# The mixed stage of a two-layer attention and expert network, with relative products, layer 1's chain and the experts' groups in another order

## The chip, the cores and the metric

The kernel runs on one core of a Trainium2 chip. The time is device microseconds (us) of one launch, median of three executions. The engines of a core are TensorE (PE in the profile, its weight loads PEld), VectorE (DVE), ScalarE (ACT), GpSimd (POOL) and SyncE (SP), which issues most DMAs. Each takes its instructions strictly in the order of its own program and waits on semaphores for the others.

## What is computed

Eight images of 32x32 tokens with 96 channels pass through a layer 0 (attention with relative position terms), a layer 1 (causal attention) and four experts, of which each token uses two:

```
x = x + conv_attn(group_norm(x))          # qkv, softmax(q k^T * scale + rel_h + rel_w) v, proj
t = t + causal_attn(layer_norm(t))        # layer 1, 6 heads of 16
scores = einsum('bsd,de->bse', x, gate_w) + gate_b       # x is now layer_norm(t)
probs  = softmax(scores); keep the top 2 of 4, divide by their sum
h = gelu(einsum('bsd,edh->ebsh', x, w1) + b1)            # 4 experts, 96 -> 384
y = einsum('ebsh,ehd->ebsd', h, w2) + b2                 # 384 -> 96
t = t + einsum('bse,ebsd->bsd', masked, y)
```

## The kernel before

One image (1024 tokens) is one element; the program is pipelined over the eight elements. For each element there is layer 1's attention (`attention(it, 1)`), the next element's layer 0 attention (`attention(it, 0)`), and then a **mixed stage**, `mix`, in which three strands of three elements run side by side:

- **rel** and **val0**, layer 0 two elements on: two groups of values (`val`), and eight relative products (`bias`, matmuls at L548 and L550, eight to a product). ScalarE copies each product out in two pieces (L980, L981), VectorE subtracts in two pieces (L1326) and frees the buffer.
- **a**, the experts of the current element: the gate (`gate_scores` L707, then `gates` on VectorE, with an Exp on ScalarE at L1012); twelve groups of `up` (L715, Gelu on ScalarE at L997) and `down` (L729), three of each to an expert; after an expert's third `down` ScalarE adds the bias (`expert_out`, L1005), TensorE transposes the result (`back`, L746) and VectorE adds it (`expert_add`, L1308).
- **next_mix**, layer 1's chain of the next element: `ln` (Ln and Exp of the softmax sums on ScalarE, L969 and L971), `den` (three steps on VectorE, L1216 to L1219), `res` (output projection L691, then residual and statistics on VectorE, L1231 to L1252), `nrm` (Ln and Exp at L869 and L871, four small steps and eight normalizing ones on VectorE, L1154 to L1258), `tr` (transposes L699, copy L986), `qk` (projections L528, ScalarE L883, VectorE L1194), `val`, `lev` (splitting in bf16 levels, L899, L1075, L1349), a write to DRAM and a read back by SyncE, and sixteen row **maxima** of layer 1's first two heads (`first_maxima`: L759 and a mask at L762, VectorE reduces at L1299).

There are nine mixed stages. Six (elements 0 to 5) hold all three strands, of which five are the turns of a hardware loop; the first of all has no experts, that of element 6 has no relative products and no val0, and the last has the experts only.

The order of the stage is one hand-written list, `MIX`; every engine walks it and executes its own part of each item. So a step that waits on one engine holds back all that stands behind it in the list on that engine. Each product, `up`, `res`, `tr`, `qk`, `val` and maximum writes a buffer of `psT`, of which there are two, used in turn (`take_mixed`): a fill waits until the fill two before it has been read, by ScalarE (`ta_free`) for `up`, `tr`, `val` and `val0`, by VectorE (`t_free`) for the others. `down` and the gate have banks of their own (`psS`, `psM`). `back` writes over the gate's bank, and the first one waits for `gates` to have finished (`m_free`). A `down` waits for its Gelu (`ta_free`). ScalarE's Gelu is in another function table than Ln and Exp; the compiler puts an ACT_TABLE_LOAD ahead of a function whose table isn't loaded.

## Time and profile before

| | before |
|---|---|
| median of 3 executions | 2429.63 us (2428.53 to 2431.78) |
| the profiled execution | 2437.21 us, of which the span is 2435.4 us |
| mean granted TensorE clock, share of 2.4 GHz | 0.878 |
| TensorE (PE) busy | 2016.1 us, 83% |
| VectorE (DVE) busy | 1238.8 us, 51% |
| ScalarE (ACT) busy | 1102.1 us, 45% |
| DMA, mean | 46 GB/s |

The profile gives for each engine the sum of its busy time. The trace gives single instructions in order of time, equal ones merged into a row; behind a row stands, in brackets, how long the engine had been idle and whose work ended that. The view of stages gives, for a stretch of time, how long each engine was busy in it and which clock TensorE was granted: 1.00 is 2.4 GHz, 0.50 is 1.2 GHz. The stage that is followed below is the mixed stage of the third turn of the loop, from 1083.92 us (its first val0 matmul) to 1179.59 us (the first matmul of the next attention).

### The profile page before, as it was taken

Reading aid. Unit: us, or ns where it says so; the run is one execution under the profiler, and the core shown is the slowest. Engines: PE = TensorE matmul, PEld = TensorE weight load, DVE = VectorE, ACT = ScalarE, POOL = GpSimd, SP = SyncE. Lnnn points to the kernel's source line nnn. Section 1 sums busy time; section 2 is a strip of 40 time slices with the busy share of each in tenths; the row PEclk is TensorE's granted clock in tenths of the full one; section 3 lists DMA queues with packets and bytes.
Section 4 is the critical chain, followed back from the end, with each engine's and each line's share of the span. In section 5 each row is a group of like instructions: output and inputs, shape, how many; then the busy total and the mean of one; then the engine's idle time right before and its main releaser. Section 6 shows DMA issues by size and latency. Waiting matters only on the chain.

```text
span 2435.4 us, 28956 instructions
## 1 busy us (share of the span) xinstructions
PE 2016.1 (83%) x9408; PEld 804.7 (33%) x9408; DVE 1238.8 (51%) x2512; ACT 1102.1 (45%) x1408; POOL 141.5 (6%) x68
## 2 busy tenths in 40 slices
PE   1389578898889988889788988889888898899858
PEld 0123222343323432334323433334323343234324
DVE  5453466454654555635664445545566355643522
ACT  0325434563445633465344643456344653455333
POOL 0000000100010000200011000100002000100010
PEclk9589669988899888999799888998899998999888
DMA  1704420243004230061202430033300621000300
GB/s 40 130 1 84 70 46 16 57 74 71 7 15 95 36 73 11 25 112 45 37 16 57 74 72 6 16 83 48 73 10 26 108 48 31 16 10 5 65 14 7
DMA packets 55740, 111.43 MB, mean 46 GB/s; under 512 B 17686, under 2 KB 18903, under 8 KB 54040
## 3 DMA queue, kind: packets, MB, share of 16 engines
q1 hardware_dynamic: 54040, 109.06, 23.2%
q8 instruction: 89, 1.46, 0.3%
q14 instruction: 75, 0.61, 0.1%
q10 hardware_dynamic: 1536, 0.30, 0.1%
HBM read 61.82 MB, written 34.60 MB: 40 GB/s over the span
## 4 chain that ended last, share of the span: by engine, by line
issue 61%; PE 21%; DVE 7%; POOL 4%; DMA 3%; SPq 2%; ACT 2%; POOLq 0%; DVEq 0%; ACTq 0%
PE psOM L612 4%; PE psS L563 4%; DVE mx L1205 4%; PE psT L591 2%; PE psT L592 2%; PE psS L729 2%; PE psT L715 2%; PE psT L594 1%; POOL split L1075 1%; PE psT L528 1%; SPq L395 1%; DMA scr<-qb 1%; DMA kb<-scr 1%; PE psT L759 1%; POOL lb L1082 1%
## 5 line engine op out<-in xcount | busy, mean ns | idle before, releaser
L944 ACT ACTIVATE probs<-psT 128x1024 f32<-128x1024 f32 (+7 forms) x768 | 624.2, 836 | 659.7 <-PE psT L592 362.5
L1205 DVE TENSOR_REDUCE mx<-psS 128x1 f32<-128x512 f32 (+3 forms) x1152 | 685.7, 641 | 461.9 <-PE psS L563 370.1
L592 PE MATMUL psT<-qb,kb 97*128 97x512 f32 x768 | 415.2, 615 | 0.0
L612 PE MATMUL psOM<-probs,v 128*32 128x512 f32 (+3 forms) x2688 | 394.2, 570 | 12.8 <-ACT probs L944 12.8
L563 PE MATMUL psS<-ka,qa 128*128 128x512 bf16 x768 | 280.1, 409 | 91.2 <-DVE mx L1205 82.4
L591 PE MATMUL psT<-qa,ka 128*128 128x512 bf16 x768 | 314.7, 410 | 29.0 <-DMA qb<-negr 28.4
L715 PE MATMUL psT<-xf,w1s 97*128 97x512 f32 x384 | 208.5, 675 | 1.6 <-DVE mrow L1299 1.6
L1326 DVE TENSOR_TENSOR qb<-psT,qa 32x768 fp32r<-32x768 f32 x128 | 121.4, 948 | 154.5 <-ACT qa L980 152.7
L729 PE MATMUL psS<-probs,w2s 128*96 128x512 f32 x384 | 192.2, 625 | 4.6 <-ACT probs L997 4.6
L997 ACT ACTIVATE probs<-psT 128x1024 f32<-128x1024 f32 x96 | 98.1, 1023 | 196.7 <-PE psT L715 196.4
L594 PE MATMUL psT<-qr,kr 97*128 97x512 bf16 (+3 forms) x576 | 183.2, 362 | 2.8 <-ACT probs L944 0.9
L563 PEld LDWEIGHTS psS<-ka,qa 128*128 128x128 bf16 x768 | 61.9, 99 | 352.4 <-DVE mx L1205 268.7
L592 PEld LDWEIGHTS psT<-qb,kb 97*128 97x128 f32 x768 | 162.5, 212 | 20.9 <-issue 2.4
L563 PE MATMUL psS<-kr,qr 96*128 96x512 bf16 (+3 forms) x384 | 137.0, 397 | 35.3 <-DVE mx L1205 31.2
L591 PEld LDWEIGHTS psT<-qa,ka 128*128 128x128 bf16 x768 | 77.8, 101 | 217.3 <-issue 134.5
L1299 DVE TENSOR_REDUCE mrow<-psT 128x1 f32<-128x128 f32 (+7 forms) x128 | 92.8, 755 | 91.3 <-PE psT L762 91.3
L612 PEld LDWEIGHTS psOM<-probs,v 128*32 128x32 f32 x2688 | 68.3, 109 | 143.9 <-issue 89.2
L759 PE MATMUL psT<-kr,qr 96*128 96x512 bf16 (+1 forms) x192 | 68.7, 440 | 56.7 <-DMA kr<-scr 30.4
L715 PEld LDWEIGHTS psT<-xf,w1s 97*128 97x128 f32 x384 | 78.3, 214 | 91.8 <-issue 78.7
L1075 POOL TENSOR_TENSOR split<-resid,split 96x1024 bf16<-96x1024 f32 x16 | 34.1, 2130 | 1224.2 <-ACT split L899 1224.2
L729 PEld LDWEIGHTS psS<-probs,w2s 128*96 128x96 f32 x384 | 63.4, 173 | 98.7 <-issue 93.4
L1308 DVE SCALAR_TENSOR_TENSOR x<-psOM,g,x 128x96 f32<-128x96 f32 x256 | 60.4, 307 | 68.7 <-PE psOM L746 68.5
(140 smaller groups left out, 1742.3 us busy)
## 6 DMA issues: line engine op xcount, KB each, us to landing
scr<-split SPq DMA_DIRECT2D x32, 576.0 KB, 4.3
scr<-qb SPq DMA_DIRECT2D x16, 768.0 KB, 4.8
qr<-scr SPq DMA_DIRECT2D x48, 192.0 KB, 6.6
au<-ot SPq DMA_DIRECT2D x192, 32.0 KB, 2.0
lb<-ot SPq DMA_DIRECT2D x192, 32.0 KB, 2.0
qr<-scr SPq DMA_DIRECT2D x48, 128.0 KB, 4.3
kr<-scr SPq DMA_DIRECT2D x48, 128.0 KB, 7.3
qa<-scr SPq DMA_DIRECT2D x32, 128.0 KB, 3.8
```

Of the source, the lines that this page charges most:

```text
L563: last = mm(bank[:, 0:n], q[0:rows, h, t * P:(t + 1) * P], k[0:rows, h, kc * HALF:kc * HALF + n], start=True, stop=not diagonal)
L591: mm(o[:, a:b], ka[:, h, ks], qa[:, h, a:b], start=True, stop=False)
L592: last = mm(o[:, a:b], kb[:, h, ks], qb[:, h, a:b], start=False, stop=True)
L594: last = mm(o[:, a:b], kr[:, h, ks], qr[:, h, a:b], start=True, stop=a != q0)
L612: last = mm(psO[j:j + 2 * HD, a - c * HALF:HALF], v[:, kt, 2 * p + hh, :], probs[:, (2 * kt + hh) % 4, a:(c + 1) * HALF], start=kt == 0, s ...
L715: last = mm(o[:, c * HALF:(c + 1) * HALF], w1s[:, a:a + P], xf[:, c * HALF:(c + 1) * HALF], start=True, stop=True)
L729: last = mm(psS[0:C, c, :], w2s[:, n, :], hbuf[:, n % 4, c * HALF:(c + 1) * HALF], start=j == 0, stop=j == HJ - 1)
L759: last = mm(o[:, c * HALF:c * HALF + n], q[0:rows, h, t * P:(t + 1) * P], k[0:rows, h, c * HALF:c * HALF + n], start=True, stop=not diagonal)
L944: A(probs[:, n % 4, q0:T], psT[:, t_slot(ts, m), q0:T], ACT.Exp).then_inc(t_free, 1)
L997: A(hbuf[:, n % 4, :], psT[:, t_slot(stage, fill), :], ACT.Gelu).then_inc(ta_free, 1)
L1205: V.reduce_max(mx[layer][:, p % 2, (h % 2) * NT + t, kc:kc + 1], psS[:, s_bank(st, fill), 0:max_cols(layer, t, kc)], AX).then_inc(s_free, 1)
L1326: ins = V.tensor_tensor(rest[0], rest[1], lead[0], ALU.subtract)
```

## The change

`MIX` is written in another order. The first six relative products no longer stand together: the list now begins rel 0, up 0, rel 1, up 1, rel 2, down 0, rel 3, and layer 1's `ln` stands behind rel 3 instead of behind rel 5. The gate moves from ahead of the first `up` to behind up 6. Ahead of the q and k projections stand ten of the experts' 24 groups, where there were thirteen; the gate and the first `back` move behind them. Between the projections and the maxima stand eight groups (seven before), and among the maxima six (three before), with two `back`s (one before); the last `back` stands behind maximum 11 instead of maximum 7.

Two waits go with it. The first `up` now waits for VectorE's copy of its input (`s_free`), which the gate did before; and ScalarE preloads the table of Ln and Exp at `ln`, since a Gelu now stands ahead of it.

```diff
-MIX = ([("val0", 0), ("val0", 1)] + [("rel", g) for g in range(6)]
-       + [("ln", 0), ("gate", 0), ("up", 0), ("up", 1), ("den", 0), ("down", 0), ("up", 2), ("rel", 6), ("down", 1), ("res", 0),
...
-       + MAXES[:2] + [("up", 11)] + MAXES[2:4] + [("down", 10)] + MAXES[4:6] + [("down", 11)] + MAXES[6:8] + [("back", 3)]
-       + MAXES[8:])
+MIX = ([("val0", 0), ("val0", 1), ("rel", 0), ("up", 0), ("rel", 1), ("up", 1), ("rel", 2), ("down", 0), ("rel", 3), ("ln", 0),
+        ("up", 2), ("rel", 4), ("down", 1), ("den", 0), ("rel", 5), ("up", 3), ("res", 0), ("down", 2), ("rel", 6), ("up", 4),
+        ("nrm", 0), ("down", 3), ("rel", 7), ("tr", 0), ("up", 5), ("qk", 0), ("qk", 1), ("val", 0), ("lev", 0), ("val", 1),
+        ("up", 6), ("gate", 0), ("down", 4), ("up", 7), ("back", 0), ("down", 5), ("up", 8), ("down", 6), ("up", 9), ("down", 7),
+        ("back", 1)]
+       + MAXES[:2] + [("down", 8)] + MAXES[2:4] + [("up", 10)] + MAXES[4:6] + [("down", 9), ("back", 2)] + MAXES[6:8]
+       + [("up", 11)] + MAXES[8:10] + [("down", 10)] + MAXES[10:12] + [("down", 11), ("back", 3)] + MAXES[12:])
...
             def up(it, stage, n):
 
+                if n == 0:
+                    pe.wait_ge(s_free, upto("s_free", it, stage, 0))
...
                     elif what == "ln":
+                        exp_table()
                         den(it, "mix")
```

The lines of the changed kernel are two or three further down than the same lines before (L715 becomes L717, L997 becomes L999, L1299 becomes L1302). Three places show what moves, all from the mixed stage of element 0, which has the same order as the loop's. First ScalarE around `ln`, before. L980 and L981 are a relative product's two copies, L969 and L971 are `ln`, L1012 is the gate's Exp, L997 a Gelu and the load of its table:

```order
L980 ACTIVATE qa<-psT 32x4x6x32
L981 ACTIVATE qa<-psT 32x192x4
L969 ACTIVATE il<-lb 96x1024
L971 ACTIVATE il<-il 96x1024
L1012 ACTIVATE g<-g 128x32
L997 ACT_TABLE_LOAD
L997 ACTIVATE probs<-psT 128x1024 x3
```

The same place on ScalarE after the change:

```order
L982 ACTIVATE qa<-psT 32x4x6x32
L983 ACTIVATE qa<-psT 32x192x4
L876 ACT_TABLE_LOAD
L971 ACTIVATE il<-lb 96x1024
L973 ACTIVATE il<-il 96x1024
L999 ACT_TABLE_LOAD
L999 ACTIVATE probs<-psT 128x1024
L982 ACTIVATE qa<-psT 32x4x6x32
L983 ACTIVATE qa<-psT 32x192x4
```

`ln` now stands between two table loads, with up 2's Gelu and rel 4's copies behind it. In a whole mixed stage ScalarE has seven table loads where it had three.

Second TensorE around the output projection L691, before, with the semaphores that each row waits for (rel 6 is ahead of these rows; L729 is a `down`, L715 an `up`):

```order
L729 MATMUL psS<-probs,w2s 96x512 [waits ta_free]
L729 MATMUL psS<-probs,w2s 96x512
L691 MATMUL psT<-wp,att 128x96 [waits ta_free,att_ready]
L691 MATMUL psT<-wp,att 128x96 x7
L715 MATMUL psT<-xf,w1s 128x512 [waits t_free]
L715 MATMUL psT<-xf,w1s 128x512
```

And after (rel 5 is ahead of these rows; L717 is up 3, L731 is down 2):

```order
L717 MATMUL psT<-xf,w1s 128x512 [waits t_free]
L717 MATMUL psT<-xf,w1s 128x512
L691 MATMUL psT<-wp,att 128x96 [waits t_free,att_ready]
L691 MATMUL psT<-wp,att 128x96 x7
L731 MATMUL psS<-probs,w2s 96x512 [waits ta_free]
L731 MATMUL psS<-probs,w2s 96x512
```

The projection's buffer was freed by ScalarE (`ta_free`, up 2's Gelu); now VectorE frees it (`t_free`, rel 5), behind `den`.

Third VectorE at the end of the stage, before: L1308 is an expert's addition (eight steps), L1299 the reductions of the maxima.

```order
L1349 TENSOR_TENSOR split<-il,split 96x1024
L1308 SCALAR_TENSOR_TENSOR x<-psOM,g,x 128x96 x16
L1299 TENSOR_REDUCE mrow<-psT 128x1 x8
L1308 SCALAR_TENSOR_TENSOR x<-psOM,g,x 128x96 x8
L1299 TENSOR_REDUCE mrow<-psT 128x1 x8
```

And after:

```order
L1311 SCALAR_TENSOR_TENSOR x<-psOM,g,x 128x96 x16
L1302 TENSOR_REDUCE mrow<-psT 128x1 x6
L1311 SCALAR_TENSOR_TENSOR x<-psOM,g,x 128x96 x8
L1302 TENSOR_REDUCE mrow<-psT 128x1 x6
L1311 SCALAR_TENSOR_TENSOR x<-psOM,g,x 128x96 x8
L1302 TENSOR_REDUCE mrow<-psT 128x1 x4
```

Two of the experts' additions now stand among the maxima where one did.

## Rows read from the trace of the kernel before

**Rows 1.** The page: busy time, share of the span, instructions of each engine.

```profile
PE 2016.1 (83%) x9408; PEld 804.7 (33%) x9408; DVE 1238.8 (51%) x2512; ACT 1102.1 (45%) x1408; POOL 141.5 (6%) x68
```

**Rows 2.** Stages: from:to, length, busy of each engine, clock, DMA share, GB/s.

```profile
1085.90:1097.80 11.90, 8.51 (x50) 3.22 (x49) 8.60 (x10) 8.47 (x11) 0.00 (x0) 0.72 0.63 114
1097.80:1105.40 7.60, 7.60 (x23) 5.30 (x23) 6.05 (x18) 5.61 (x7) 0.00 (x0) 0.53 0.03 2
1105.40:1133.70 28.30, 28.30 (x101) 13.04 (x100) 15.27 (x43) 16.37 (x20) 0.00 (x0) 1.00 0.00 1
1133.70:1155.00 21.30, 18.75 (x70) 9.14 (x69) 8.45 (x19) 10.14 (x12) 2.12 (x1) 1.00 0.37 103
1155.00:1177.20 22.20, 17.29 (x60) 6.65 (x60) 13.29 (x24) 2.39 (x3) 0.00 (x0) 0.68 0.62 100
```

**Rows 3.** Order of time, first relative products: start, length, instruction, idle before.

```profile
1085.87 0.26 PE L548 MATMUL psT<-qr,relt 96*32 96x192 bf16 x1
...
1087.37 0.80 ACT L980 ACTIVATE qa<-psT 32x768 bf16<-32x768 f32 x1 [0.90 <-PE psT L550]
...
1088.20 3.85 DVE L1326 TENSOR_TENSOR qb<-psT,qa 32x768 fp32r<-32x768 f32 x4 [7.40 <-ACT qa L980]
...
1090.16 0.26 PE L548 MATMUL psT<-qr,relt 96*32 96x192 bf16 x1 [1.54 <-DVE qb L1326]
```

**Rows 4.** Order of time, ScalarE: `ln`'s second step, and the table load of `nrm`.

```profile
1100.62 1.06 ACT L971 ACTIVATE il<-il 96x1024 f32<-96x1024 f32 x1
...
1123.04 1.28 ACT L874 ACT_TABLE_LOAD   x1
1124.33 0.21 ACT L869 ACTIVATE sm<-sm 128x8 f32<-128x8 f32 x1
```

**Rows 5.** Order of time: a `down`, an `up`, its Gelu, a `back` at full clock.

```profile
1106.56 1.88 PE L729 MATMUL psS<-probs,w2s 128*96 128x512 f32 x4
...
1108.28 1.88 PE L715 MATMUL psT<-xf,w1s 97*128 97x512 f32 x4
...
1110.20 1.02 ACT L997 ACTIVATE probs<-psT 128x1024 f32<-128x1024 f32 x1 [2.41 <-PE psT L715]
...
1123.51 0.83 PE L746 MATMUL psOM<-cst,xg 96*128 96x96 f32 x8
```

**Rows 6.** Order of time, layer 1's chain; the first row from the first mixed stage.

```profile
271.48 3.73 PE L691 MATMUL psT<-wp,att 97*128 97x96 f32 x16 [5.30 <-DVE att L1219]
...
1108.01 1.22 DVE L1219 SCALAR_TENSOR_TENSOR att<-il,au 96x1024 f32<-96x1024 f32 x1
...
1113.27 1.92 PE L691 MATMUL psT<-wp,att 97*128 97x96 f32 x16
...
1118.48 0.17 DVE L1252 TENSOR_SCALAR sm<-sm 128x8 f32<-128x8 f32 x1
...
1125.62 2.01 DVE L1258 TENSOR_SCALAR xn_tok<-x,sm 128x96 f32<-128x96 f32 x8
```

**Rows 7.** Order of time, the gate on TensorE and the last step of `gates`.

```profile
1097.78 3.58 PE L707 MATMUL psOM<-gw,xf 97*128 97x4 f32 x16
...
1105.18 0.19 DVE L1291 TENSOR_TENSOR g<-g,gden 128x32 f32<-128x32 f32 x1
```

**Rows 8.** Order of time, TensorE, the first of the maxima.

```profile
1154.98 0.23 PE L759 MATMUL psT<-kr,qr 96*128 96x128 bf16 x1 [2.55 <-DMA kr<-scr]
```

**Rows 9.** Order of time, VectorE in the maxima: an addition and four reductions.

```profile
1168.77 1.88 DVE L1308 SCALAR_TENSOR_TENSOR x<-psOM,g,x 128x96 f32<-128x96 f32 x8
...
1173.03 1.73 DVE L1299 TENSOR_REDUCE mrow<-psT 128x1 f32<-128x640 f32 x2 [0.25 <-PE psT L762]
1174.98 2.24 DVE L1299 TENSOR_REDUCE mrow<-psT 128x1 f32<-128x896 f32 x2 [0.22 <-PE psT L762]
```

**Rows 10.** Order of time, element 6's mixed stage: `ln`, and the first reductions.

```profile
2211.05 1.06 ACT L969 ACTIVATE il<-lb 96x1024 f32<-96x1024 f32 x1 [6.34 <-DMA lb<-ot]
...
2264.08 0.62 DVE L1299 TENSOR_REDUCE mrow<-psT 128x1 f32<-128x128 f32 x2 [2.69 <-PE psT L762]
```

More of the change, by code:

```diff
@@ L69 @@
 MAXES = [("max", i) for i in range(2 * NT)]
-MIX = ([("val0", 0), ("val0", 1)] + [("rel", g) for g in range(6)]
-       + [("ln", 0), ("gate", 0), ("up", 0), ("up", 1), ("den", 0), ("down", 0), ("up", 2), ("rel", 6), ("down", 1), ("res", 0),
-          ("up", 3), ("down", 2), ("rel", 7), ("up", 4), ("down", 3), ("nrm", 0), ("back", 0), ("up", 5), ("down", 4),
-          ("up", 6), ("tr", 0), ("down", 5), ("up", 7), ("qk", 0), ("qk", 1), ("down", 6), ("val", 0), ("lev", 0), ("val", 1),
-          ("back", 1), ("up", 8), ("down", 7), ("up", 9), ("down", 8), ("up", 10), ("back", 2), ("down", 9)]
-       + MAXES[:2] + [("up", 11)] + MAXES[2:4] + [("down", 10)] + MAXES[4:6] + [("down", 11)] + MAXES[6:8] + [("back", 3)]
-       + MAXES[8:])
+MIX = ([("val0", 0), ("val0", 1), ("rel", 0), ("up", 0), ("rel", 1), ("up", 1), ("rel", 2), ("down", 0), ("rel", 3), ("ln", 0),
[5 more added lines that the diff above has]
+       + [("up", 11)] + MAXES[8:10] + [("down", 10)] + MAXES[10:12] + [("down", 11), ("back", 3)] + MAXES[12:])
 def there(stage, kind):
```

## The prediction, made before the changed kernel ran

> **What bounds the kernel now.** I read the page first, then the stages of one turn, then the order of time within them. TensorE is busy 83% of the span, VectorE 51% and ScalarE 45% [rows 1], so TensorE's time is the kernel's time, and the question is where it idles or runs at the lower clock. In the mixed stage that is two places [rows 2]. In the six relative products (1085.9 to 1097.8) TensorE works 8.5 of 11.9 us, and its clock falls from 1.00 to 0.50 there, so that the gate and the first two `up`s behind them run at 0.53. From the first maximum to the last (1155.0 to 1177.2) it works 17.3 of 22.2 us at a mean clock of 0.68. In between lie 28 us without a gap at 1.00, and a wait of 2.55 us for layer 1's keys to come back from DRAM [rows 8]. The change puts experts' groups into both thin places. The two weak places cost at most some 3.4 us of idle time, 3.5 us of low clock, 2.6 us of waiting and 5 us idle among the maxima; what has to be asked is what the new neighbours wait for.
>
> **Prices.** A relative product takes TensorE 1.3 us. The first one starts at 1085.87, ScalarE's two copies of 0.80 start 1.50 us later, VectorE's two subtractions (1.92 us, half of the 3.85) end at 1090.12, and TensorE takes the buffer again at 1090.16, 4.29 us after the start [rows 3]. An `up` or `down` takes 1.72 us at full clock (1106.56 to 1108.28), and the Gelu starts 1.92 us after its `up` and lasts 1.02; a `back` takes 0.8 [rows 5]. A table load takes 1.28 us and the next instruction starts 0.01 later [rows 4]. `ln` is two steps of 1.06 [rows 4]. `den` is three steps of 1.22, so 3.7 us; `res` takes TensorE 1.8 us at full clock (1113.27) and 3.7 at half (271.48), and residual and statistics end 3.6 us after its matmuls (1115.03 to 1118.65); `nrm` takes VectorE 2.8 us, the last 2.01 of them in one row [rows 6]. `gates` ends 4.0 us after the gate's last matmul (1101.36 to 1105.37); that gate took 3.58 us at half clock, so I take 1.9 at full [rows 7]. An expert's addition takes 1.88 us [rows 9]. The last four of a head's eight reductions take 1.73 and 2.24 a pair [rows 9].
>
> **Part 1, up to the projections of q and k.** I lay the new order out by these prices, from 0 at the first val0 matmul (1083.92); a fill can't start before the fill two places ahead of it is read. Products at 1.95, 6.24 and 10.53 alternate with `up`s at 3.25 and 7.54: TensorE waits 1.27 us ahead of each, because a pair of product and `up` fills 3.0 of the 4.29 us. That is no better than two products in 4.3 us before, only more work in it. Rel 3 runs at 13.55, up 2 at 14.85. Now ScalarE: rel 3's copies end at 16.7; then load, Ln, Exp, load (4.7 us), so up 2's Gelu ends at 22.4, rel 4's copies, which wait behind it though their matmuls ended at 19.1, at 24.1, and VectorE is done with rel 4 at 25.2. `den` follows (to 29.0), then rel 5's subtractions (to 30.9). The output projection needs `den` and the buffer of rel 5: it starts at 31.0, while rel 5 and up 3, the last work ahead of it, ended at 27.0. So TensorE does 3.0 us of work from 20.9 to 31.0. Then `res` to 32.7, down 2, rel 6, up 4, down 3 and rel 7 to 40.5. Up 4's Gelu, the load and Ln/Exp of `nrm` end at 40.4, VectorE's `nrm` at 43.3, `tr` starts there (2.8 us of waiting), rel 7 is freed at 45.2, up 5 runs to 47.0, and the projections start at 47.0. Before they started at 49.8 (the edge of the stages at 1133.7, [rows 2]), but with three more groups (5.2 us), the gate and a `back` done.
>
> **Part 2, to the first maximum.** The projections take 3.4 us, the two `val`s 1.9 and 1.5 of waiting for VectorE, since no `down` stands between them any more; then eight groups (13.8), the gate (1.9) and two `back`s (1.6). The first `back` waits for `gates`: VectorE starts these after `lev`, which ends at 57.1, and the gate's Exp has ended by 58.4, so `gates` is done at 61.7 and TensorE idles 0.8. Sum 25.0: the first maximum starts at 72.0. Before it started at 71.1 (1154.98) [rows 8]. The transfer took 21.3 us from the projections [rows 2, 8], so the data is there at 68.3 and the 2.55 us wait is gone; what takes its place is TensorE's own work. At full clock this half is 0.9 us longer.
>
> **Clock of part 1.** In the relative products before, the clock fell after stretches in which TensorE worked 8.5 of 11.9 us [rows 2]. The stretch from 20.9 to 31.0 is much emptier (3.0 of 10.1), so I take the low clock for `res` (+1.9 by the 3.7 us at 271.48 [rows 6]) and for down 2 (+1.7, double its 1.72); both lie on the chain to `nrm`. That is +3.6. Bounds: 0 if the clock holds, and +5.4 if it has fallen already in the first pairs, which adds up 2's and down 1's delay to `ln`'s chain.
>
> **Part 3, the maxima.** Before, 22.2 us at a mean clock of 0.68 [rows 2]. After, from 0 again: back 1's addition first (to 2.0), maxima 0 and 1, down 8, maxima 2 and 3; up 10 waits for max 2's reduction (3.5 to 5.2); max 5 waits for up 10's Gelu (6.4); down 9, back 2, maxima 6 and 7 to 10.3; but VectorE does the addition first (to 11.4), so up 11 gets its buffer at 12.6; max 9 waits for up 11's Gelu (15.6); down 10, maxima 10 and 11, down 11 to 19.7; back 3 waits 1 us for ScalarE's `expert_out`, which stands directly ahead of it, and ends at 21.5; then the addition (23.5) and the last four reductions (0.8 + 0.9 + 2.24) to 27.6. So +5.4 us. VectorE's own work is 13.3 us [rows 2] plus two more additions, 17.1; TensorE has six groups and two `back`s, 12 us, beside the maxima: the two buffers make them take turns instead of overlapping. Ends: +2.4 if some 3 us of these turns overlap after all, and 3.4 more than my value if up 11 and down 10 run at half clock; I take neither, since the maxima now start out of dense work.
>
> **The added table loads.** Four per stage, 5.1 us of ScalarE; two are in `ln`'s 4.7 us above, one in `nrm`'s. First the row: from the load at 1123.04 the next instruction starts at 1124.33 [rows 4]. The Trainium skill, page "ScalarE: Activation LUTs", section "What ACT_TABLE_LOAD costs", gives 1283 ns for the load, as this trace, but 2.66 us for a switch with its drain, and its rules say to do all of one set before switching, which speaks against this change. By its figure the three loads on the chain would cost 4.1 us more a stage; this trace doesn't bear out the drain.
>
> **Sum.** A full stage: 0.9 + 3.6 + 5.4 = +9.9, six times: +59.4. The first stage has no groups; its chain starts two products earlier but pays a load: -1. In element 6's stage `ln` waits 6.34 us for its DMAs [rows 10] with the gate's Exp and two Gelus queued behind it; these Gelus now come first. The same count gives the first maximum 8.1 us earlier than before (reductions from 2264.08 [rows 10]), less 3 for low clock after `nrm`'s wait, and +5.4 in the maxima: +0.3. The last stage: the first `back` waits 0.6 for `gates`: +0.6. Total +59.3. The profiled execution was 2437.2, which gives 2496.5; it lies 7.6 above the median of 2429.6, so the median comes to 2489.
>
> **Rivals.** (a) The same waits but the clock holds in part 1: for it, `up`s are dense work and 28 us of groups ran at 1.00 [rows 2]; against it, the ten empty us. Six times 6.3, -1, -2.7, +0.6: +34.7, so 2464. (b) The clock falls in the first pairs and among the maxima too, where 0.68 stands now [rows 2]: six times (1.8 + 3.4) = 31 more: 2520. (c) Faster: the pairing works as meant. VectorE would have to get through `den` and rel 5 without TensorE waiting, so that of part 1's waits only the 1.27s and the 0.8 of `tr`'s buffer are left: 7 us less and no low clock, 0.9 + 5.4 - 7.7 = -1.4 a stage, with -3 elsewhere -11: 2418. It decides on whether the wait ahead of `res` and `tr` together stays under 0.5 us; `ln`'s 4.7 us on ScalarE [rows 4] speak against it. (d) A switch costs more than its row: if each of the three loads on the chain held ScalarE as long again as its 1.28, 3.8 us in each of 7 stages: 27 more, 2516; against it, the start 0.01 us behind the load [rows 4]. (The Trainium skill's page on ScalarE, same section, would make it so.) (e) Nothing measurable, where the gains in clock balance the maxima: 2430.
>
> **How the numbers follow.** Forecast 0.50, (a) 0.22, (b) 0.12, (c) 0.10, (d) 0.02, (e) 0.04. The range takes the forecast, (a) and (b) with some room for the size of the stage terms: 2450 to 2523; it leaves out (c) and (e). 0.2% is about what a measurement of this kernel can tell from no change. Faster 0.10, same 0.04, slower 0.86.
>
> **What would show it.** In the changed trace of a loop's stage: waits of TensorE of about 1.3 us for VectorE's subtraction ahead of rel 1, 2 and 4; some 4 us idle ahead of L691, ended by VectorE; about 2.8 ahead of L699; no wait for a DMA at the first maximum, and that maximum 75 to 76 us after the first val0; 27 to 28 us from first to last maximum; clock 0.5 around L691. I am wrong if the projection's wait is under 1 us, or if the maxima take less than 24 us.

## The result, and the profile after

The changed kernel takes 2536.0 us (median of 4 runs, 2529.1 to 2545.8), the kernel before on the same chip 2430.7 (2428.5 to 2432.2): a ratio of 1.0437 with a 95% interval of 1.0401 to 1.0473. The direction is the forecast one, but the loss is 105 us where 59 were worked out, and the time lies 13 us above the range. The profiled executions span 2527.2 and 2435.4 us.

The page's line of busy times stands beside [rows 1]: TensorE is busy for 29 us more in 92 us more span, VectorE the same, ScalarE 44 us more (31 table loads more, 1.28 us each, are 40 of these).

```profile
PE 2045.4 (81%) x9408; PEld 803.0 (32%) x9408; DVE 1239.4 (49%) x2512; ACT 1146.2 (45%) x1439; POOL 141.6 (6%) x68
```

I follow element 2's stage, that of [rows 2] (the third of the six full stages, and the second turn of the loop, not the third as is said ahead of the prediction). It begins with the first val0 matmul, at 1083.92 before and 1107.61 after; times with a plus sign count from there. First the windows of the kernel before (from:to, length, busy time of TensorE, weight loads, VectorE, ScalarE and GpSimd, granted clock, DMA share, GB/s): up to the first maximum, and the whole stage up to the transpose of the maxima. Then the same of the changed kernel, with the maxima between.

```profile
1083.92:1154.98 71.06, 65.12 (x254) 32.57 (x253) 38.36 (x89) 41.67 (x51) 2.12 (x1) 0.90 0.25 54
1083.92:1179.60 95.68, 82.43 (x315) 39.25 (x313) 51.67 (x113) 44.06 (x54) 2.12 (x1) 0.84 0.33 63
```

```profile
1107.61:1186.17 78.56, 65.89 (x234) 30.33 (x233) 34.67 (x73) 44.89 (x52) 2.13 (x1) 0.87 0.28 56
1186.17:1216.50 30.33, 21.88 (x82) 8.90 (x80) 16.99 (x40) 4.78 (x6) 0.00 (x0) 0.84 0.29 53
1107.61:1219.04 111.43, 87.76 (x314) 39.24 (x313) 51.67 (x113) 49.67 (x58) 2.13 (x1) 0.85 0.28 54
```

The stage grew by 15.75 us with the same matmuls in it. TensorE's busy time grew by 5.3 of these, its idle time by 10.4 (13.25 to 23.67). The mean granted clock of the stage is nearly what it was (0.84 and 0.85): the low clock lies at other places, and for longer in all. So the clock explains only part of the 5.3. The rest fits the rows ahead of waits: an `up` there shows 1.98 us of busy time, where in a dense stretch the next instruction starts after 1.72, and there are more waits now. It wasn't split further. By halves: 71.06 to 78.56 us up to the first maximum, 22.24 to 30.33 from there to the last reduction.

The order of time of TensorE in that stage (start, length, instruction, idle time ahead of it and what ended it), changed kernel:

```profile
1113.85 0.26 PE L548 MATMUL psT<-qr,relt 96*32 96x192 bf16 x1 [0.92 <-DVE qb L1329]
...
1133.15 3.78 PE L717 MATMUL psT<-xf,w1s 97*128 97x512 f32 x4 [1.31 <-DVE qb L1329]
1138.85 3.73 PE L691 MATMUL psT<-wp,att 97*128 97x96 f32 x16 [1.92 <-DVE qb L1329]
1142.37 3.36 PE L731 MATMUL psS<-probs,w2s 128*96 128x512 f32 x4
...
1154.83 1.27 PE L699 MATMUL psT<-cst,xn_tok 128*96 128x128 f32 x8 [2.70 <-DVE xn_tok L1261]
1156.70 3.78 PE L717 MATMUL psT<-xf,w1s 97*128 97x512 f32 x4 [0.59 <-DVE qb L1329]
...
1186.17 0.22 PE L761 MATMUL psT<-kr,qr 96*128 96x128 bf16 x1
...
1198.61 2.50 PE L717 MATMUL psT<-xf,w1s 97*128 97x512 f32 x4 [2.06 <-DVE mrow L1302]
...
1202.53 3.67 PE L731 MATMUL psS<-probs,w2s 128*96 128x512 f32 x4
```

Three things are to be seen. Rel 1 starts at +6.24, the output projection (L691) at +31.2, and ahead of them TensorE waits for VectorE's subtractions; up 3, between rel 5 and the projection, already runs at half clock (3.78). The projection and down 2 behind it take 3.73 and 3.36 us, where before they took 1.92 and 1.88; up 5, behind the wait for `nrm`, takes 3.78 too. The first maximum waits for no DMA any more, but among the maxima down 10 takes 3.67 us, and up 11 ahead of it 2.50, the lower clock again.

Element 1's stage, from 806.73, shows that the low clock doesn't come at the same places every time. TensorE from the first pairs to the maxima:

```profile
814.35 3.78 PE L717 MATMUL psT<-xf,w1s 97*128 97x512 f32 x4
...
819.45 3.73 PE L731 MATMUL psS<-probs,w2s 128*96 128x512 f32 x4
...
840.55 3.73 PE L691 MATMUL psT<-wp,att 97*128 97x96 f32 x16 [1.92 <-DVE qb L1329]
...
858.66 3.78 PE L717 MATMUL psT<-xf,w1s 97*128 97x512 f32 x4
...
888.67 0.22 PE L761 MATMUL psT<-kr,qr 96*128 96x128 bf16 x1
...
901.11 1.98 PE L717 MATMUL psT<-xf,w1s 97*128 97x512 f32 x4 [2.06 <-DVE mrow L1302]
```

and VectorE's last reductions in it:

```profile
912.12 4.14 DVE L1302 TENSOR_REDUCE mrow<-psT 128x1 f32<-128x640 f32 x4
```

Here up 1 and down 0 run at half clock among the first pairs, and the first maximum comes at +81.9 instead of +78.6. Up 11 takes 1.98 us behind the same wait of 2.06, so the maxima run at the full clock nearly to their end and take 27.6 us, not 30.3. In the six full stages, in order, the first maximum comes at +82.2, 81.9, 78.6, 82.0, 78.2 and 79.5 (mean 80.4; before 71.7), and the maxima take 29.3, 27.6, 30.3, 27.6, 30.3 and 30.3 us (mean 29.2; before 22.0).

The table gives the length of every mixed stage, from ScalarE's last copy of the attention's output to its copy of `negb` for the next attention (the last stage: to the end of the span), in us:

| | first | el. 0 | 1 | 2 | 3 | 4 | 5 | el. 6 | last |
|---|---|---|---|---|---|---|---|---|---|
| before | 73.9 | 96.3 | 95.2 | 96.1 | 97.0 | 94.3 | 93.8 | 82.4 | 89.7 |
| after | 73.6 | 112.0 | 112.9 | 111.8 | 112.4 | 111.4 | 110.2 | 83.3 | 88.5 |

A full stage has gone from 95.4 to 111.8 on average: +16.4, six times 98. The first, element 6's and the last changed by -0.3, +0.9 and -1.2. What is left, some -6, lies outside the mixed stages, in parts that the change doesn't touch. The profiled execution is also the fastest of the changed kernel's four (2529.1, the others up to 2545.8), so the medians stand 105 apart and the two profiles 92.

### The profile page after: what moved, and what is told of

The parts are those of the page before. It is cut to its first block, busy times and chain, and to the rows that moved or that the text cites. A ratio compares the mean times of both kernels' runs of the same rounds, so it can differ in the third digit from the quotient of the medians.

```text
span 2527.2 us, 28993 instructions
## 1 busy us (share of the span) xinstructions
PE 2045.4 (81%) x9408; PEld 803.0 (32%) x9408; DVE 1239.4 (49%) x2512; ACT 1146.2 (45%) x1439; POOL 141.6 (6%) x68
## 4 chain that ended last, share of the span: by engine, by line
PE 63%; DVE 17%; ACT 6%; issue 6%; DMA 5%; SPq 1%; POOL 1%; DVEq 0%; POOLq 0%; ACTq 0%
PE psOM L612 12%; PE psS L563 10%; DVE mx L1208 8%; PE psT L591 7%; PE psT L592 7%; PE psT L717 6%; PE psS L731 5%; PE psT L594 3%; PE psT L528 3%; DMA qb<-negr 2%; DVE qb L1329 2%; DVE x L1311 1%; DVE mrow L1302 1%; PE psT L550 1%; ACT probs L999 1%
## 5 line engine op out<-in xcount | busy, mean ns | idle before, releaser
L717 PE MATMUL psT<-xf,w1s 97*128 97x512 f32 x384 | 218.2, 698 | 25.9 <-DVE mrow L1302 16.2
L731 PE MATMUL psS<-probs,w2s 128*96 128x512 f32 x384 | 206.5, 665 | 0.0
L999 ACT ACTIVATE probs<-psT 128x1024 f32<-128x1024 f32 x96 | 98.2, 1024 | 176.6 <-PE psT L717 176.3
L563 PE MATMUL psS<-kr,qr 96*128 96x512 bf16 (+3 forms) x384 | 135.0, 390 | 35.2 <-DVE mx L1208 31.2
L1302 DVE TENSOR_REDUCE mrow<-psT 128x1 f32<-128x128 f32 (+7 forms) x128 | 92.9, 754 | 67.0 <-PE psT L764 66.5
L717 PEld LDWEIGHTS psT<-xf,w1s 97*128 97x128 f32 x384 | 76.3, 213 | 127.6 <-issue 80.7
L1007 ACT ACTIVATE xg<-psS,b2s 96x512 f32<-96x512 f32 x64 | 43.6, 683 | 114.1 <-PE psS L731 112.9
L761 PE MATMUL psT<-kr,qr 96*128 96x512 bf16 (+1 forms) x192 | 58.7, 381 | 43.3 <-DVE mrow L1302 16.6
```

What stands on the lines that cost most here:

```text
L563: last = mm(bank[:, 0:n], q[0:rows, h, t * P:(t + 1) * P], k[0:rows, h, kc * HALF:kc * HALF + n], start=True, stop=not diagonal)
L717: last = mm(o[:, c * HALF:(c + 1) * HALF], w1s[:, a:a + P], xf[:, c * HALF:(c + 1) * HALF], start=True, stop=True)
L731: last = mm(psS[0:C, c, :], w2s[:, n, :], hbuf[:, n % 4, c * HALF:(c + 1) * HALF], start=j == 0, stop=j == HJ - 1)
L999: A(hbuf[:, n % 4, :], psT[:, t_slot(stage, fill), :], ACT.Gelu).then_inc(ta_free, 1)
L1302: V.reduce_max(mrow[:, 0, n:n + 1], psT[:, t_slot(st, fill), 0:cols], AX).then_inc(t_free, 1)
```

## The experiments

All are timed in alternation with the kernel before on the same chip (its medians: 2431.5, 2432.0 and 2435.3 us in the three groups of runs), in at least four executions. "Stage" is the mean of the six full stages, counted as in the table.

### Spare matmuls in TensorE's waits

The changed kernel, with eleven matmuls whose result nobody reads in each full stage: one ahead of rel 1, 2, 4 and 5 and of up 3, three ahead of `res`, three ahead of `tr`.

```diff
+            def keep_busy(it):
+                pe.wait_ge(o_free, upto("o_free", it, "mix", 0))
+                mm(psO[:, :], w1s[:, 0:P], xf[:, 0:HALF], start=True, stop=True)
...
+                extra = {("rel", 1): 1, ("rel", 2): 1, ("rel", 4): 1, ("rel", 5): 1, ("up", 3): 1, ("res", 0): 3, ("tr", 0): 3}
```

> The changed kernel, with eleven spare matmuls (97x512 f32, 0.86 us each at full clock, into a bank that nothing uses there) in the full mixed stages, placed where TensorE waits: one ahead of rel 1, rel 2, rel 4, rel 5 and up 3, three ahead of res and three ahead of tr. They add work and no wait; the result is the same. Theory A (low clock after the stage's waits is what my sum missed): no low clock at up 3, res, down 2, up 5 and the projections, so about 6 us less in each of six stages although 9.5 us of work is added: 2490 to 2505 against 2536. Rival B (the waits themselves are longer than laid out, the clock matters little): the spare matmuls gain nothing or cost: 2536 to 2560.

Measured: 2503.9 us (2497.0 to 2504.3), 1.0303 of before (1.0276 to 1.0329). With more work the kernel is 32 us faster than without it. Element 0's stage (up to the first maximum, and the maxima), then element 2's up to the first maximum:

```profile
506.35:580.28 73.93, 67.87 (x256) 30.74 (x255) 34.67 (x73) 44.75 (x52) 2.13 (x1) 1.00 0.34 63
580.28:607.91 27.63, 18.95 (x82) 8.14 (x80) 16.96 (x40) 4.78 (x6) 0.00 (x0) 0.96 0.28 54
1087.42:1161.35 73.93, 69.11 (x256) 31.11 (x255) 34.67 (x73) 44.86 (x52) 2.13 (x1) 0.98 0.32 61
```

In element 2's stage the mean clock is 0.98 where the changed kernel had 0.87, and the first maximum comes at +73.9 instead of +78.6, though TensorE is busy 3.2 us longer. The eleven take some 9.5 us (0.86 each, an estimate: each is half an `up`, which takes 1.72), so all other matmuls together take 6.3 us less (65.89 to 59.6): that much at most the low clock had cost up to there, for the fuller waits also cut the 0.26 us at the ends of rows. `res` takes 2.02 us here and up 5 1.98; down 2 still runs low (3.29). Element 0's stage is the clearest: at full clock the changed order needs 73.9 and 27.6 us, where the changed kernel took this stage in 82.2 and 29.3.

Not all of the 32 us lies where the matmuls were added. In the two profiles the six full stages take 107.8 instead of 111.8 us on average, 24 us less in all; element 6's, which has no spare matmuls, takes 11 more, and the attention stages, which have none either, take 21 less. How long the low clock lasts in those parts differs from trace to trace.

### The same in two halves

The last three of the eleven alone (ahead of `tr`), and the first eight alone.

```diff
+                extra = {("tr", 0): 3}
```

> The changed kernel with 3 spare matmuls ahead of the transposes alone (of the 11 of the first experiment), in full stages. Of the 32 us that all 11 gave back, theory A puts some 3 us a stage on the transposes' wait (up 5 and the projections at half clock): 2512 to 2525 us. Rival J (what matters is the first half of the stage): 2530 or more.

```diff
+                extra = {("rel", 1): 1, ("rel", 2): 1, ("rel", 4): 1, ("rel", 5): 1, ("up", 3): 1, ("res", 0): 3}
```

> The complement: the changed kernel with the other 8 spare matmuls, 5 at the products' waits and 3 ahead of the residual, none at the transposes. Theory A: down 2 and rel 6 behind the residual go at the full clock, about 3 us a stage: 2510 to 2525 us. With the run beside it the two gains add up to about the 32 us of all 11. Rival K (the clock only falls later then): 2530 or more.

Measured: 2538.3 us (2522.4 to 2547.6), 1.0436 (1.0411 to 1.0460) with the three; 2517.0 (2512.6 to 2524.6), 1.0329 (1.0308 to 1.0351) with the eight. The eight give back 19 us (26 by the ratios), as expected; the three give nothing, against my expectation of 11 to 24 us. Together that is less than the 32 us of all eleven, but each ratio is known to within a quarter to a third of a percent, 6 to 9 us, so the sum is neither shown nor refuted. TensorE in the kernel with the three, in order of time (its lines are five further down: L696 is `res`, L704 `tr`, L722 `up`):

```profile
1141.10 3.73 PE L696 MATMUL psT<-wp,att 97*128 97x96 f32 x16 [1.92 <-DVE qb L1338]
...
1157.34 1.07 PE L704 MATMUL psT<-cst,xn_tok 128*96 128x128 f32 x8
1159.21 1.98 PE L722 MATMUL psT<-xf,w1s 97*128 97x512 f32 x4 [0.79 <-DVE qb L1338]
1161.03 3.60 PE L528 MATMUL psT<-xnt,wqkv 96*96 96x512 f32 x8
```

and with the eight:

```profile
1140.44 1.92 PE L696 MATMUL psT<-wp,att 97*128 97x96 f32 x16
...
1153.18 1.94 PE L704 MATMUL psT<-cst,xn_tok 128*96 128x128 f32 x8 [2.70 <-DVE xn_tok L1270]
...
1158.62 5.32 PE L528 MATMUL psT<-xnt,wqkv 96*96 96x512 f32 x8
```

Each does at its own place what it was put there for: with the three, the fall behind the 2.70 us wait is gone (up 5 1.98, projections 3.60) and `res` runs at half; with the eight it is the other way round, `res` 1.92 (though up 3 ahead of it still takes 3.41), transposes and most of the projections at half. In the profiled execution the kernel with the three is indeed shorter in five of the six stages (109 us, the six together 12 us), but element 6's, without spare matmuls, takes 90.4 us instead of 83.3, and that execution (2522.4) is 14 to 25 us shorter than its other three. So the mechanism is seen at `tr`; that it is worth something there by itself, the times don't show.

### No change of function table

Gelu is replaced by Copy, which needs no table, and the preloads of the table of Ln and Exp are dropped (at `ln`, at `nrm` and at layer 1's attention); in the changed kernel, and the same in the kernel before. Both leave Gelu out, and a Copy takes the same 1.02 us.

```diff
-                A(hbuf[:, n % 4, :], psT[:, t_slot(stage, fill), :], ACT.Gelu).then_inc(ta_free, 1)
+                A(hbuf[:, n % 4, :], psT[:, t_slot(stage, fill), :], ACT.Copy).then_inc(ta_free, 1)
```

> The changed kernel with a plain copy in place of Gelu and without the table preloads behind the first, so that ScalarE never changes its table (the Gelu is left out). To be read against the same edit of the kernel before. Theory A: the four added loads explain only part, about 3.9 us a stage through ln and nrm: this one keeps some 60 to 80 of the 105 us difference to its counterpart. Rival C (the added table loads are what makes the change slow): the difference to the counterpart falls under 30 us.

> The kernel before with a plain copy in place of Gelu and without the later table preloads (the Gelu is left out): the counterpart. All theories: 2400 to 2430, since its loads lie mostly beside TensorE's work; the one at each attention's start and the one ahead of the first Gelu may give 1 to 2 us a stage.

Measured: 2517.4 us (2498.9 to 2526.0), 1.0353 (1.0292 to 1.0414) for the changed kernel; 2429.9 (2421.3 to 2438.3), 0.9996 (0.9978 to 1.0014) for the one before. With one load left in the whole program (63 and 32 otherwise) the change still costs 87 us of its 105. The loads are left with some 18 us, 2.6 for each of seven stages, less than the three of 1.28 that I had put on the chain. The executions of the first of the two spread over 27 us, and the intervals of the ratios leave anything from nothing to some 36 us; rival (d) needs 54, twice the 27 of the three rows. Before, three loads a stage are worth nothing that these runs can tell (groups stand beside them).

### The new maxima alone

The order of before up to up 9, and from there the changed order, with six groups and two `back`s among the maxima.

```diff
-          ("back", 1), ("up", 8), ("down", 7), ("up", 9), ("down", 8), ("up", 10), ("back", 2), ("down", 9)]
-       + MAXES[:2] + [("up", 11)] + MAXES[2:4] + [("down", 10)] + MAXES[4:6] + [("down", 11)] + MAXES[6:8] + [("back", 3)]
-       + MAXES[8:])
+          ("back", 1), ("up", 8), ("down", 7), ("up", 9)]
+       + MAXES[:2] + [("down", 8)] + MAXES[2:4] + [("up", 10)] + MAXES[4:6] + [("down", 9), ("back", 2)] + MAXES[6:8]
+       + [("up", 11)] + MAXES[8:10] + [("down", 10)] + MAXES[10:12] + [("down", 11), ("back", 3)] + MAXES[12:])
```

> The kernel before with only the last part changed: six groups and two backs among the maxima, as the change has them, instead of three and one; up to back 1 as before. Theory A (two buffers make TensorE and VectorE take turns, and the first maximum waits for its data, not for the groups that were ahead of it): the maxima take 28 to 30 us instead of 22, the wait for DRAM ahead of them grows from 2.5 to 8 us: 6 to 8 us more a stage in seven stages, 2475 to 2490. Rival D (groups among the maxima fill idle time there, and the loss is in the first part): 2430 or less.

Measured: 2506.1 us (2496.2 to 2517.8), 1.0316 (1.0268 to 1.0364): 75 us, where 44 to 58 were expected (2475 to 2490). The first maximum didn't move, since it hangs on the DMA, and the work that had stood ahead of it now follows it:

```profile
1169.39 0.29 PE L759 MATMUL psT<-kr,qr 96*128 96x128 bf16 x1 [8.46 <-DMA kr<-scr]
```

That is +71.94 from this stage's start at 1097.45; before it was +71.06, with a wait of 2.55 [rows 8]. The maxima take 32.2 us from there to the last reduction, against 22.2; some of that is the low clock, for in the changed kernel they took 27.6 without it. So groups don't fill the maxima. They are taken from a place where they filled a wait for a DMA, and put where TensorE and VectorE take turns over two buffers.

### The first part alone

The changed order up to back 1, then the order of before: up 10, down 8, back 2 and down 9 ahead of the maxima, three groups and a `back` among them.

> The changed list up to back 1, and then the list of before: up 10, down 8, back 2, down 9, the maxima with three groups among them. Theory A (both parts of the move cost, each mainly through TensorE's low clock behind its waits): four operations go back ahead of the maxima, where they fill the DMA wait; TensorE's own work is the same, and of the maxima's 5 to 8 us of growth some 2 to 6 us a full stage go away: 2495 to 2525 us against 2536 of the change. Rival E (all of the loss lies in the first part, the maxima only inherit it): within 10 us of the change, 2526 to 2546. Rival F (the growth of the maxima is most of it, as the run of before with the new maxima, 2506, could be read): 76 us less, 2455 to 2475.

Measured: 2515.8 us (2505.6 to 2522.0), 1.0342 (1.0300 to 1.0385): 20 us less than the changed kernel, as theory A had it. No full stage waits for the DMA at the first maximum, and the maxima take 19.2 to 19.6 us. Its list:

```diff
-        ("back", 1)]
-       + MAXES[:2] + [("down", 8)] + MAXES[2:4] + [("up", 10)] + MAXES[4:6] + [("down", 9), ("back", 2)] + MAXES[6:8]
-       + [("up", 11)] + MAXES[8:10] + [("down", 10)] + MAXES[10:12] + [("down", 11), ("back", 3)] + MAXES[12:])
+        ("back", 1), ("up", 10), ("down", 8), ("back", 2), ("down", 9)]
+       + MAXES[:2] + [("up", 11)] + MAXES[2:4] + [("down", 10)] + MAXES[4:6] + [("down", 11)] + MAXES[6:8] + [("back", 3)]
+       + MAXES[8:])
```

The first part costs 84 us, the new maxima 75, both together 105. They overlap: in the changed kernel the first part delays TensorE so far that the DMA is no longer waited for, so the new maxima don't add that wait. It grew by 5.9 us (2.55 to 8.46) in element 2's stage of the run above, six times 35 us of the 54 by which the two sum to more than the whole; the rest isn't accounted for.

### Only the pairs

The pairing of the first six products alone; from `ln` on the order of before, minus what was paired.

```diff
-MIX = ([("val0", 0), ("val0", 1)] + [("rel", g) for g in range(6)]
-       + [("ln", 0), ("gate", 0), ("up", 0), ("up", 1), ("den", 0), ("down", 0), ("up", 2), ("rel", 6), ("down", 1), ("res", 0),
+MIX = ([("val0", 0), ("val0", 1), ("rel", 0), ("up", 0), ("rel", 1), ("up", 1), ("rel", 2), ("down", 0), ("rel", 3),
+        ("up", 2), ("rel", 4), ("down", 1), ("rel", 5), ("ln", 0), ("gate", 0), ("den", 0), ("rel", 6), ("res", 0),
```

> The changed kernel's first pairs alone (rel 0, up 0, rel 1, up 1, rel 2, down 0, rel 3, up 2, rel 4, down 1, rel 5), and from the statistics on the list of before, its gate, its chain at its old place, its maxima. Theory A (the loss of the first part comes from waits that no group fills, and here three ups and two downs are no longer there to stand behind rel 5): the first pairs save nothing, because each rel waits for VectorE's bf16 copies, and the groups are missing between rel 5 and the residual: 2 to 6 us a full stage, 2443 to 2467 us. Rival H (pairing is free, since groups fill the waits between rels): 2425 to 2440. Rival I (pairing is the whole loss of the first part, as large as the run with the old maxima, 2516): 2500 or more.

Measured: 2501.3 us (2498.2 to 2514.2), 1.0288 (1.0256 to 1.0321): 66 us, more than twice the 8 to 32 of theory A. Rival I's 2500 holds, just; but the pairs are 66 us of the first part's 84, not the whole. Where they go, in element 2's stage, from 1102.30 (order of time, VectorE's last step of `den` and the first four matmuls of `res`):

```profile
1138.87 1.22 DVE L1222 SCALAR_TENSOR_TENSOR att<-il,au 96x1024 f32<-96x1024 f32 x1
...
1140.22 1.17 PE L691 MATMUL psT<-wp,att 97*128 97x96 f32 x4 [9.25 <-DVE att L1222]
```

TensorE stands still for 9.25 us ahead of the output projection, whose sixteen matmuls then take 3.73 us. The chain from `ln` through `gates` and `den` is as long as before (9.4 us from ScalarE's Ln at 1130.67, before 9.7 from 1099.54). Before, between rel 5 and `res`, TensorE had the gate, three `up`s, two `down`s and rel 6 and never waited ([rows 7], [rows 5], and `res` at full clock at 1113.27, [rows 6]); here it has the gate and rel 6. The pairs fill waits of 0.5 to 1.5 us with the groups that had covered this chain. The changed kernel softens this by starting `ln` two products earlier: its two waits there are 1.31 and 1.92.

### Real work in the two long waits

The changed kernel with down 2 ahead of `res` and down 4 ahead of `tr`.

```diff
-        ("up", 2), ("rel", 4), ("down", 1), ("den", 0), ("rel", 5), ("up", 3), ("res", 0), ("down", 2), ("rel", 6), ("up", 4),
-        ("nrm", 0), ("down", 3), ("rel", 7), ("tr", 0), ("up", 5), ("qk", 0), ("qk", 1), ("val", 0), ("lev", 0), ("val", 1),
-        ("up", 6), ("gate", 0), ("down", 4), ("up", 7), ("back", 0), ("down", 5), ("up", 8), ("down", 6), ("up", 9), ("down", 7),
+        ("up", 2), ("rel", 4), ("down", 1), ("den", 0), ("rel", 5), ("up", 3), ("down", 2), ("res", 0), ("rel", 6), ("up", 4),
+        ("nrm", 0), ("down", 3), ("rel", 7), ("down", 4), ("tr", 0), ("up", 5), ("qk", 0), ("qk", 1), ("val", 0), ("lev", 0), ("val", 1),
+        ("up", 6), ("gate", 0), ("up", 7), ("back", 0), ("down", 5), ("up", 8), ("down", 6), ("up", 9), ("down", 7),
```

> The changed kernel with down 2 moved ahead of the residual's product and down 4 ahead of the transposes, so that the 1.9 and 2.7 us waits there hold real work (0.86 to 1.0 us of matmuls each). Theory A (the waits and the low clock behind them are the loss): the waits shrink by the work moved in, about 1.8 us a stage, and where the clock then holds 2 to 4 us more: 2500 to 2525 us. If it is data that comes late whatever TensorE does in between, and the clock has no part: 1.8 us times 6 at most, 2525. If moving them delays ScalarE's and VectorE's chain instead: 2536 or more.

Measured: 2512.8 us (2510.4 to 2514.2), 1.0341 (1.0304 to 1.0377): 23 us less than the changed kernel. TensorE at the two places, and where down 4 was taken from (L748 is `back` 0, L731 behind it down 5), in order of time:

```profile
1135.45 1.92 PE L691 MATMUL psT<-wp,att 97*128 97x96 f32 x16
...
1146.39 1.08 PE L699 MATMUL psT<-cst,xn_tok 128*96 128x128 f32 x8 [0.23 <-DVE xn_tok L1261]
1148.33 1.98 PE L717 MATMUL psT<-xf,w1s 97*128 97x512 f32 x4 [0.86 <-DVE qb L1329]
1150.15 3.60 PE L528 MATMUL psT<-xnt,wqkv 96*96 96x512 f32 x8
...
1165.01 1.54 PE L748 MATMUL psOM<-cst,xg 96*128 96x96 f32 x8 [2.20 <-DVE g L1294]
1166.34 3.14 PE L731 MATMUL psS<-probs,w2s 128*96 128x512 f32 x4
```

From this stage's start at 1103.62 the transposes come at +42.8 instead of +47.2, although a `down` more lies ahead of them, and `res`, the transposes, up 5 and the projections run at full clock. The gain is less than that. Down 4 had covered `back` 0's wait for `gates`, which is now 2.20 us instead of 0.83, with the low clock behind it (down 5 takes 3.14); and the maxima here fall to the low clock in every full stage (up 11 takes 3.76 us in this one).

### Up 11 ahead of the maxima

The same idea in the kernel before, whose one wait there is that for layer 1's keys [rows 8]: up 11 moves ahead of the first maximum, down 10, down 11 and back 3 move one place forward.

```diff
-          ("back", 1), ("up", 8), ("down", 7), ("up", 9), ("down", 8), ("up", 10), ("back", 2), ("down", 9)]
-       + MAXES[:2] + [("up", 11)] + MAXES[2:4] + [("down", 10)] + MAXES[4:6] + [("down", 11)] + MAXES[6:8] + [("back", 3)]
+          ("back", 1), ("up", 8), ("down", 7), ("up", 9), ("down", 8), ("up", 10), ("back", 2), ("down", 9), ("up", 11)]
+       + MAXES[:2] + [("down", 10)] + MAXES[2:4] + [("down", 11)] + MAXES[4:6] + [("back", 3)] + MAXES[6:8]
```

> The kernel before with up 11 moved from among the maxima to ahead of the first of them, where TensorE waits for a DMA; down 10, down 11 and back 3 each one place earlier. Theory A (a wait that holds work costs no clock): the 2.6 us wait shrinks to some 0.7 to 0.9, up 11 is no longer at half clock (3.8 to 1.9 us), and the maxima are bound by VectorE's reductions only: 1.5 to 4 us less for each of 6 stages, 2405 to 2424 us against 2431. Rival G (the maxima are bound by VectorE alone, up 11 lay hidden beside it): no change, 2426 to 2436.

And for the clock's share, three spare matmuls at that place, nothing moved:

```diff
+                if i == 0:
+                    for _ in range(3 if kind_of(it) in ("second", "body") else 0):
+                        mm(o[:, 0:HALF], w1s[:, 0:P], xf[:, 0:HALF], start=True, stop=True)
+                    pe.wait_ge(l1_first, upto("l1_first", it, "mix", 192))
```

> The kernel before with 3 spare matmuls (512 columns, results overwritten) ahead of the first maximum in full stages, in the maximum's own buffer, while the DMA is awaited. Nothing else is moved. Theory A (the clock falls because TensorE stands still there): up 11 and what follows go at the full clock more often, 0.5 to 3 us less a stage, 2413 to 2428 us, about as far as moving up 11 there less the work moved. Rival G (the maxima are bound by VectorE's reductions): 2430 to 2436. Both read with the run that moves up 11: if that is faster and this is not, it is the work moved that pays, not the clock.

> The kernel before with up 11 ahead of the maxima (2400) and 2 spare matmuls besides in what is left of the DMA wait, 0.74 us. Theory A: with the wait nearly gone there is no clock left to save, and the two matmuls end about when the DMA does: 2395 to 2408 us, the same as with up 11 alone. If the fall at the start of the maxima went away too: 2390 or less.

Measured: 2400.1 us (2398.3 to 2402.1), **0.9882 of before (0.9847 to 0.9918)**, with up 11 moved; 2416.8 (2405.4 to 2424.2), 0.9940 (0.9918 to 0.9962), with the spare matmuls; 2405.4 (2402.6 to 2411.1), 0.9885 (0.9867 to 0.9903), with up 11 and two spare ones. The first is faster than both kernels of this case. TensorE in the kernel before, up 11 and down 10 behind the first maxima:

```profile
1155.65 3.37 PE L715 MATMUL psT<-xf,w1s 97*128 97x512 f32 x4 [0.21 <-DVE mrow L1299]
...
1160.64 3.05 PE L729 MATMUL psS<-probs,w2s 128*96 128x512 f32 x4
```

The same with the spare matmuls (L755) ahead of the first maximum (L763):

```profile
1137.35 2.74 PE L755 MATMUL psT<-xf,w1s 97*128 97x512 f32 x6
1139.93 0.22 PE L763 MATMUL psT<-kr,qr 96*128 96x128 bf16 x1
...
1140.59 1.98 PE L715 MATMUL psT<-xf,w1s 97*128 97x512 f32 x4 [0.21 <-DVE mrow L1301]
...
1143.98 1.91 PE L729 MATMUL psS<-probs,w2s 128*96 128x512 f32 x4
```

And with up 11 moved:

```profile
1141.95 1.88 PE L715 MATMUL psT<-xf,w1s 97*128 97x512 f32 x4
1144.58 0.23 PE L759 MATMUL psT<-kr,qr 96*128 96x128 bf16 x1 [0.74 <-DMA kr<-scr]
```

The spare matmuls fill the wait and the first maximum isn't late (+71.07, as before), but up 11 takes 1.98 us instead of 3.37 and down 10 1.91 instead of 3.05. That is 2.5 us of matmul time behind a wait of 2.55, and 15 us over the program: the clock behind this wait cost about as much as the wait. (The profile is of the fastest of this kernel's ten executions.) In all six full stages the maxima take 19.0 to 19.5 us here. With up 11 itself in the wait, they take 17.6 us instead of 22.2 (1144.58 to 1162.23), though the first comes 1.6 us later. Compared over the profiles' full stages, the spare matmuls save 3.2 us a stage (95.4 to 92.2) and up 11 in the wait 4.0 (91.4), so most of the gain there is the clock's. Up 11 is also moved in element 6's stage, 82.4 to 77.3 us, where nothing spare was added (82.5). More matmuls in the 0.74 us that are left add nothing.

## Why the prediction was right about the direction and wrong about the size

**The waits: right.** The layout had rel 1 and rel 2 at 6.24 and 10.53, `res` at 31.0 and, with the clock's 3.6 for all behind `res`, the transposes at 46.9. They start at +6.24 and +10.53, +31.24 and +47.22 in element 2's stage. (The idle time in front of rel 1 shows as 0.92 us, not 1.27, since the `up` ahead of it has a row of 1.98 us and was counted with 1.72.) The wait for a DMA at the first maximum is gone. Of the signs for the waits one doesn't hold as written: ahead of L691 the trace shows 1.92 us, not some 4. The layout had up 3 end at 27.0; it starts on time, at +25.5 behind a wait of 1.31 for rel 4's buffer, but at half clock takes 3.78 us and fills 1.8 of the four. So the low clock began ahead of up 3, where it cost nothing yet.

**Part 3: right where its condition held.** The maxima were to take 27.6 us at full clock. In element 1's stage they do: 888.67 to 916.26. In element 2's they take 30.3, where up 11 and down 10 run low; this is near the outer end of my range for the part (+3.4), which I had set aside "since the maxima now start out of dense work". They do start at full clock; the fall comes 12 us later, around the wait of 2.06 us ahead of up 11, which in element 1's stage brings none. The +5.4 is also a difference of unlike things: the 22.2 us held much low clock, the 27.6 hardly any. Nearly at full clock the old maxima take 19.0 (the run with three spare matmuls), so the turns over two buffers cost 8.6 us, and 3.2 of them were paid by clock that the old order had lost.

**The clock: the step that failed.** I took +3.6 in part 1, for `res` and down 2 alone, and nothing in part 3. These two come out as worked (3.73 and 3.36 to 3.62 us). What I left out: the wait of 2.7 ahead of `tr`, which I had in my sum as idle time, has the same effect on what is behind it: up 5, and the projections, +3 us (first maximum at +78.56 for 75.6). And it falls among the first pairs in element 1's stage (up 1, down 0: +3.3 up to the first maximum) or among the maxima in element 2's (+2.7). So these two stages close with 0.9 for the waits, 5.4 for the maxima and 9.9 and 9.3 for the clock:

| | worked out | element 1 | element 2 |
|---|---|---|---|
| first maximum at full clock | 72.0 | | |
| `res` and down 2 | +3.6 | +3.6 | +3.6 |
| up 5 and projections | 0 | +3.0 | +3.0 |
| first pairs | 0 | +3.3 | 0 |
| first maximum | 75.6 | 81.9 | 78.6 |
| maxima | 27.6 | 27.6 | 30.3 |

(The 3.3 are what is left of 81.9 after the others; 2.6 of them are there at `res` already, at +33.8 for +31.2. The 3.0 are 78.6 less 75.6.) Over all six stages the first maximum comes at 80.4 on average and the maxima take 29.2, which is 4.8 and 1.6 us more than the 75.6 and 27.6; six times 6.4 are 38 of the 39 us by which the sum was short in the profile's stages (98 against 59). That it is the clock, and not a longer wait, element 0's stage shows: 82.2 and 29.3 us in the changed kernel, 73.9 and 27.6 with the spare matmuls at a clock of 1.00 and 0.96.

**From the stages to the median.** The sum gave 2496.5 for a profiled execution and took 7.6 off for the median, as before. The profiled execution took 2529.1, 33 us more, and lies 7 below its median instead of 8 above. So 14 of the 47 us between 2489 and 2536 come from that last step, which was a guess about which execution would be profiled.

**The rivals.** (b) came nearest in mechanism, "the clock falls in the first pairs and among the maxima too", 2520; the trace shows the one place or the other, in element 0's stage both, and `tr` besides, which (b) left out. With a chance of 0.12 it stood too low, and (a), the clock holds, with 0.22 too high: the trace of before had the evidence, a wait of 2.55 us [rows 8] with a clock of 0.68 behind it [rows 2], which I had read as a property of the maxima. The spare matmuls there show that up 11's and down 10's share of it hangs on the wait. (c) fell by its own test: 1.92 and 2.70 us ahead of `res` and `tr`, where it allowed 0.5 together. (d), loads that cost twice their row, fell by the runs without tables; the Trainium skill, page "ScalarE: Activation LUTs", section "What ACT_TABLE_LOAD costs", has 2.66 us for a switch, but these runs leave 2.6 us a stage for four added loads together, and in the changed kernel's trace `ln`'s Exp ends at 1127.99 us, the load behind it starts at 1128.01 and the Gelu behind the load at 1129.30. So the measurement doesn't bear that figure out here.

**The ends.** First, element 6's and last stage were put at -1, +0.3 and +0.6; they came to -0.3, +0.9 and -1.2.

**What stays open.** Why the clock falls here in one stage and there in the next, with the same order, wasn't found. It does so in the kernel before too: in element 4's stage the maxima take 19.5 us behind the same wait, in the others 22.2 to 23.7. The executions differ too (the shortest of the changed kernel's at a mean clock of 0.880, the longest at 0.875): its four spread over 17 us, those of the kernel before over 4 beside it, but over 14 and 22 us in the two larger groups of runs. So a difference of a few us between two profiles says nothing by itself. Nor was it tested what moving the gate costs alone.

## What to carry to other kernels

Work that "fills a thin place" is taken from another place. Before moving it, ask which chain it covers where it stands: the pairs, by themselves, filled waits of 1 us and uncovered one of 9. Where a trace shows half clock behind a wait of TensorE, count that as part of the wait's price, and apply it to every such wait in the new order, as a range: in these traces the same wait brought it in one stage and not in the next. Moving one piece of real work into the wait can pay twice (here 1.2% for one `up`). A few spare matmuls are a cheap test of the clock's share: they move nothing, and whatever they gain was clock. Compare medians and every stage, for one stage of one profile can show the fall elsewhere.

## What was not expected of the hardware

Adding eleven unread matmuls to each of six stages, 9.5 us of TensorE's work a stage by the estimate above, made the changed kernel 1.3% faster (2536.0 to 2503.9), the granted clock up to the first maximum rising from 0.87 to 0.98 in element 2's stage. In element 6's stage, where nothing was added, the same kernel took 94.7 us instead of 83.3, at a mean clock of 0.80 instead of 0.94: the clock's falls move even where the code is the same.
